# Windowed attention in a decoder: scores and values as one 64-row, 32-column matmul per head

## What is computed

```python
for i in range(DEPTH):                                   # 6 layers
    x = attn_layer(shift_tokens(x), Wqkv[i], q_scale[i], k_scale[i], Wo[i]) + x
    x = ffn_layer(shift_tokens(x), ln_g[i], ln_b[i], W1[i], b1[i], W2[i], b2[i]) + x

def attn_layer(x, Wqkv, qs, ksc, Wo):
    q, k, v = jnp.split(x @ Wqkv, 3, -1)                 # 16 heads of 64
    q, k = l2norm(q) * qs, l2norm(k) * ksc               # then rotary tables on both
    out = local_attention(q, k, v)
    return out @ Wo

def local_attention(q, k, v):                            # windows of 32, keys of this window and the last
    sim = jnp.einsum('bhwie,bhwje->bhwij', bq, bk2) * QK_SCALE
    attn = jax.nn.softmax(jnp.where(mask, -max, sim), -1)
    return jnp.einsum('bhwij,bhwje->bhwie', attn, bv2)
```

## Time and profile before

| | us |
|---|---|
| median of 3 runs | 2283.92 (2264.66 to 2285.11) |
| the profiled execution | 2264.08 |
| its span, first to last instruction | 2262.3 |
| PE busy | 2027.8 (90%) |
| DVE busy | 1530.3 (68%) |
| ACT busy | 1326.9 (59%) |
| POOL busy | 995.1 (44%) |
| mean granted TensorE clock | 0.962 of full speed |

### The profile page before, as it was taken

One profiled execution on the slowest core, in us unless ns is written; L12 is line 12 of the kernel. 1 busy time (PEld: TensorE's weight loads), 2 busy tenths in 40 slices (PEclk: granted clock), 3 DMA queues, 4 the chain that ended last, 5 costly groups with the idle time before them and its releaser, 6 DMA issues. The chain is left out here.

```text
span 2262.3 us, 46768 instructions
## 1 busy us (share of the span) xinstructions
PE 2027.8 (90%) x19016; PEld 1170.9 (52%) x19016; DVE 1530.3 (68%) x1741; ACT 1326.9 (59%) x1857; POOL 995.1 (44%) x715
## 2 busy tenths in 40 slices
PE   6799887589999999999999999999999999999996
PEld 2122133246656565555655565656555565556553
DVE  3989225466777677677777777767767777777762
ACT  3057764355665566656665666556665666566653
POOL 6000003165555555555555555555555555555540
PEclk8589998789999999999999999999999999999998
DMA  4510000034333343333443334433344333333331
GB/s 110 101 20 2 2 18 16 25 93 123 84 94 92 101 121 105 101 87 96 130 105 92 87 97 113 112 92 93 93 120 116 89 101 95 92 94 100 94 89 41
DMA packets 102357, 194.55 MB, mean 86 GB/s; under 512 B 12400, under 2 KB 32368, under 8 KB 102000
## 3 DMA queue, kind: packets, MB, share of 16 engines
q1 hardware_dynamic: 102144, 191.56, 32.4%
HBM read 123.77 MB, written 54.66 MB: 79 GB/s over the span
## 5 line engine op out<-in xcount | busy, mean ns | idle before, releaser
L1212 POOL TENSOR_TENSOR l_rot<-l_rot,l_rot_s 128x1024 f32<-128x1024 f32 x192 | 459.9, 2396 | 89.7 <-ACT l_norms L1413 64.9
L1527 DVE TENSOR_TENSOR l_rot<-ps,l_tab_c 128x1024 f32<-128x1024 f32 x192 | 235.2, 1225 | 313.2 <-PE ps L1248 195.5
L1215 POOL TENSOR_TENSOR l_rot<-l_rot,l_norms 128x1024 f32<-128x1024 f32 x192 | 365.3, 1903 | 15.1
L1201 POOL COPY l_kb<-l_kb 128x512 f32<-128x512 f32 x95 | 57.9, 610 | 709.4 <-ACT l_kb L1427 709.4
L1401 ACT ACTIVATE l_sq<-ps 128x1024 f32<-128x1024 f32 x192 | 196.8, 1025 | 221.7 <-PE ps L1239 219.1
L1539 DVE TENSOR_TENSOR l_rot_s<-ps,l_tab_s 128x512 f32<-128x512 f32 x384 | 245.6, 681 | 0.0
L1290 PE MATMUL ps<-l_vb,l_pT 128*32 128x128 f32 x6144 | 187.0, 273 | 65.0 <-ACT l_pT L1393 65.0
L1518 DVE TENSOR_REDUCE l_norms<-l_sq 128x16 f32<-128x1024 f32 x192 | 232.2, 1209 | 0.0
L1239 PE MATMUL ps<-l_wqkv,xsT 128*128 128x512 f32 x384 | 188.4, 615 | 26.6 <-ACT l_v_tok L1393 15.3
L1290 PEld LDWEIGHTS ps<-l_vb,l_pT 128*32 128x32 f32 x6144 | 165.9, 110 | 82.2 <-ACT l_pT L1393 82.2
L1410 ACT ACTIVATE l_norms<-l_norms 128x16 f32<-128x16 f32 x192 | 41.5, 216 | 279.6 <-POOL l_norms L1209 279.1
(11 more groups left out here) (165 smaller groups left out, 3352.1 us busy)
## 6 DMA issues: line engine op xcount, KB each, us to landing
l_vb<-v_scratch SPq DMA_DIRECT2D x336, 256.0 KB, 4.6
v_scratch<-l_v_tok SPq DMA_DIRECT2D x96, 512.0 KB, 4.8
l_vb<-v_scratch SPq DMA_DIRECT2D x48, 192.0 KB, 3.1
xsT<-xT SPq DMA_DIRECT2D x48, 135.8 KB, 2.5
stack<-scratch SPq DMA_DIRECT2D x96, 64.0 KB
l_xf<-xT SPq DMA_DIRECT2D x48, 128.0 KB, 2.3
l_wqkv_odd<-wqkv SPq DMA_DIRECT2D x9, 512.0 KB, 6.5
scratch<-parts SPq DMA_DIRECT2D x4, 768.0 KB, 11.4
```

What stands on the lines that cost most here:

```text
L1212: nc.gpsimd.tensor_tensor(rot[:, n], rot[:, n], rot_s[:, n], ALU.add).then_inc(added, 1)
L1215: nc.gpsimd.tensor_tensor(rot[:, n], rot[:, n], norms[:, t % 2, n, :, None].broadcast_to([P, HEADS, DH]), ALU.mult).then_inc(rotated, 1)
L1527: nc.vector.tensor_tensor(rot[:, 1 - r], slot(name, t).rearrange("p n (h d) -> p (n h) d", d=DH), tab_c[:, 1 - r, t % TILES, None, :].broa ...
```

## The change

`kb` and `vb` lose the parity axis: both heads' keys lie in the same columns, one head in partitions 0 to 63 and the other in 64 to 127, without zeros. `scores` and `values` issue two matmuls where one was, one per head, each with 64 rows, 32 columns and 64 moving columns; the even heads go to the slot's first bank and the odd heads to its second. The readers of these banks on DVE take the heads in the new order, and write `l_dif` and `l_o_tok` in the old one. The DMAs that spread v have the same source, size and number; their destination has no gap for the other parity. ACT copies kT with one ACTIVATE of 128 partitions, and takes the inverse norm of k behind the square of q and the copy of the probabilities.

```diff
-                    kb=sb("l_kb", [P, 2, PAIRS, 2, WINDOW + P]), vb=sb("l_vb", [P, WINDOWS, 2, PAIRS * DH]))
+                    kb=sb("l_kb", [P, 2, PAIRS, WINDOW + P]), vb=sb("l_vb", [P, WINDOWS, PAIRS * DH]))
...
-                            sp.dma_start(vb[r:r + WINDOW, j:, a, :], src.rearrange("(j r) x -> r j x", r=WINDOW))\
+                            sp.dma_start(vb[r:r + WINDOW, j:, :], src.rearrange("(j r) x -> r j x", r=WINDOW))\
...
-                    nc.gpsimd.tensor_copy(kb[:, t % 2, :, :, 0:WINDOW],
-                                          kb[:, (t - 1) % 2, :, :, P:P + WINDOW]).then_inc(carried, 1)
+                    nc.gpsimd.tensor_copy(kb[:, t % 2, :, 0:WINDOW],
+                                          kb[:, (t - 1) % 2, :, P:P + WINDOW]).then_inc(carried, 1)
...
                         for j in range(WINDOWS):
-                            a = j * WINDOW
-                            m = nc.tensor.matmul(dst[a:a + WINDOW, c // 4, (c % 4) * P:(c % 4 + 1) * P],
-                                                 qT[:, c, a:a + WINDOW], kb[:, t % 2, c, :, a:a + 2 * WINDOW],
-                                                 start=False, stop=True, skip_group_check=True)
+                            a, at = j * WINDOW, 2 * c * WINDOW
+                            for n in range(2):
+                                rows = slice(64 * n, 64 * n + 64)
+                                m = nc.tensor.matmul(dst[a:a + WINDOW, n, at:at + 2 * WINDOW],
+                                                     qT[rows, c, a:a + WINDOW], kb[rows, t % 2, c, a:a + 2 * WINDOW],
+                                                     start=False, stop=True, skip_group_check=True)
...
                         for j in range(WINDOWS):
-                            a = j * WINDOW
-                            m = nc.tensor.matmul(dst[a:a + WINDOW, c // 4, (c % 4) * P:(c % 4 + 1) * P],
-                                                 pT[:, c, a:a + WINDOW], vb[:, j, :, c * DH:(c + 1) * DH],
-                                                 start=True, stop=True, skip_group_check=True)
+                            a, cols = j * WINDOW, slice(c * DH, (c + 1) * DH)
+                            for n in range(2):
+                                rows = slice(64 * n, 64 * n + 64)
+                                m = nc.tensor.matmul(dst[a:a + WINDOW, n, cols], pT[rows, c, a:a + WINDOW],
+                                                     vb[rows, j, cols], start=True, stop=True, skip_group_check=True)
...
-                    src = slot("kT", t).rearrange("p n (c q) -> p (n c) q", q=P)
-                    for parity in range(2):
-                        rows = slice(64 * parity, 64 * parity + 64)
-                        m = nc.scalar.activation(kb[rows, t % 2, :, parity, WINDOW:], src[rows, :, :], ACT.Copy)
-                    m.then_inc(emptied("kT", t), 1)
+                    nc.scalar.activation(kb[:, t % 2, :, WINDOW:],
+                                         slot("kT", t).rearrange("p n (c q) -> p (n c) q", q=P), ACT.Copy)\
+                        .then_inc(emptied("kT", t), 1)
...
                     if has(t):
-                        inverse_norm(t, 0)
                         square(t, 1)
                     if has(t - 2):
                         copy_probs(t - 2)
+                    if has(t):
+                        inverse_norm(t, 0)
...
-                    nc.vector.tensor_tensor(dif[:, :, :], s,
-                                            mx[:, t % 2, :, None].broadcast_to([P, HEADS, 2 * WINDOW]),
+                    nc.vector.tensor_tensor(dif[:, :, :].rearrange("p (c n) k -> p n c k", n=2), s,
+                                            mx[:, t % 2, :, :, None].broadcast_to([P, 2, PAIRS, 2 * WINDOW]),
                                             ALU.subtract).then_inc(emptied("s", t), 1)
...
-                    nc.vector.tensor_tensor(o_tok[:, :, :], slot("o", t).rearrange("p n (h d) -> p (n h) d", d=DH),
-                                            inv[:, t % 2, :, None].broadcast_to([P, HEADS, DH]), ALU.mult)\
+                    nc.vector.tensor_tensor(o_tok[:, :, :].rearrange("p (c n) d -> p n c d", n=2),
+                                            slot("o", t).rearrange("p n (c d) -> p n c d", d=DH),
+                                            inv[:, t % 2, :].rearrange("p (c n) -> p n c", n=2)[:, :, :, None]
+                                            .broadcast_to([P, 2, PAIRS, DH]), ALU.mult)\
```

More of the change, by code:

```diff
@@ L834, in _ @@
                 pool.memset(env["xsT"][:, :, 0:1], 0.0).then_inc(zeroed, 1)
-                pool.memset(kept["kb"][:, :, :, :, :], 0.0).then_inc(zeroed, 1)
-                pool.memset(kept["vb"][:, :, :, :], 0.0).then_inc(zeroed, 1)
+                pool.memset(kept["kb"][:, :, :, :], 0.0).then_inc(zeroed, 1)
+                pool.memset(kept["vb"][:, :, :], 0.0).then_inc(zeroed, 1)
                 for t in range(NT):
@@ L986, in layers @@
         qT = sb("l_qT", [P, PAIRS, P])
-        mx = sb("l_mx", [P, 2, HEADS])
+        mx = sb("l_mx", [P, 2, 2, PAIRS])
         dif = sb("l_dif", [P, HEADS, 2 * WINDOW])
@@ L1556, in shift_scores @@
                 def shift_scores(t):
-                    s = slot("s", t).rearrange("p n (h k) -> p (n h) k", k=2 * WINDOW)
+                    s = slot("s", t).rearrange("p n (c k) -> p n c k", k=2 * WINDOW)
                     wait_full(dve, "s", t)
-                    nc.vector.tensor_reduce(mx[:, t % 2, :], s, AX.X, ALU.max).then_inc(maxed, 1)
+                    nc.vector.tensor_reduce(mx[:, t % 2], s, AX.X, ALU.max).then_inc(maxed, 1)
                     wait(dve, maxed, t + 1)
                     wait(dve, exped, t)
-                    nc.vector.tensor_tensor(dif[:, :, :], s,
-                                            mx[:, t % 2, :, None].broadcast_to([P, HEADS, 2 * WINDOW]),
+                    nc.vector.tensor_tensor(dif[:, :, :].rearrange("p (c n) k -> p n c k", n=2), s,
+                                            mx[:, t % 2, :, :, None].broadcast_to([P, 2, PAIRS, 2 * WINDOW]),
                                             ALU.subtract).then_inc(emptied("s", t), 1)
```

## The result

The changed kernel takes 2371.86 us (median of 4 runs, 2362.1 to 2377.82), the kernel before, run beside it, 2280.06 us (2264.66 to 2285.11). The ratio is 1.041, with a 95% interval of 1.0345 to 1.0476. It is slower by 4.1%, where 2112 us were forecast. The profiled execution took 2375.76 us.

What follows compares the result with a forecast made beforehand. PE was taken as the bound, with a small hole per step from ScalarE's order. Four steps sum to -6.45 us per batch, x 24 = -155: 2109, stated as 2112 us; own range 2085 to 2140, 8-in-10 range 2080 to 2225.

Steps and rivals of the forecast that it cites:

- So PE issues a pair in 7 to 11 ns: Scores and values on PE: issue time per load and matmul, read from bursts of eight weight loads.
- 128 x 8.5 = 1.09: New scores or values group: 128 pairs at 8.5 ns, plus 0.06 handover, 1.15 us; 1.33 us saved per step.
- no burst in the trace is longer than eight: Point noted in favour of a limit by instruction issue or fetching, in PE's scores and values.
- rival 2: Scores and values: instruction issue or fetching keeps each pair at 28 ns; 3.6 us per group, 2545 us; chance 0.16.
- 28 x 4 = 112: Scores and values: 112 ns nearly equals a 128-column pass, 109 ns, so columns explain the cost without a per-pair price.
- pT wait gone: PE's wait before values for ScalarE's copy of turned probabilities, 65.0 us in all, vanishes when the k norm moves.
- Row halves at the same time: Scores and values on PE: both 64-row halves of a column group run together; array bound 0.9 us per group.
- Rival 1: Scores and values: row halves take turns or PE looks ahead too little; groups stay 1.76 us, 2199 us; chance 0.18.
- One copy of kT: ScalarE: one 128-partition copy replaces two of 64 partitions, removing 1.03 us.
- The carry: POOL's carry moves half the elements: 0.61 us becomes some 0.33, bounds 0.3 and 0.61.
- The new order of reads on DVE, 0: DVE's maxima, differences and scaled outputs: same element count, so 0 change, bounds -0.1 and +0.3 us each.
- Late next in the hidden layer: Hidden layer step: PE's second group waits for DVE to free the scores' bank; 1.31 us stall, -0.88 left.

Runs made afterwards that it cites:

- e12: Changed kernel with the v projection moved between scores and values on PE (a repeat run): 2192.84 us, ratio 0.9632 to the kernel before.
- e5: Kernel before with the norm of k behind the pT copy and each scores and values matmul split in two of 64 columns: 2389.71 us, ratio 1.0484.
- half columns: Kernel before with the norm of k behind the pT copy, only even heads' scores and values computed: 2132.51 us, single run.

## Why the prediction was wrong

**The step that failed** is the one from a burst to a group: "So PE issues a pair in 7 to 11 ns", read from eight loads, and then "128 x 8.5 = 1.09". The rate within a group came out nearly so, 10 ns per pair. What fell is that a group gets its instructions at that rate. In its place the runs showed a supply of about 27 ns per pair over a page, and 207 us of stalls in 113 gaps; eight pairs are 16 of the 256 instructions of a page and could never show it. The text had the warning ("no burst in the trace is longer than eight") and gave rival 2 0.16.

**Rival 2** had the right cause by name ("fetching instructions") and side, in the wrong form. It made every pair take 28 ns, 3.6 us a group, 2545 us. In fact a group runs at 10 ns per pair until the page ends, and PE then stands, 1.84 us in the mean of the 113 gaps; with the eight records of the v projection between the dense groups (e12) 45 gaps with 41 us are left. So the loss is 207 us of stalls, not 2 x 1.8 x 96 = 346. My case against the rival, that 28 x 4 = 112 is the column price, was right (the runs with 64 columns show it) and didn't bear on it: the supply's 27 ns stood right beneath it, and the array's price hid it. The page of 256 instructions could be read in the trace of before, from q8's packets beside PE's records, and I didn't read it; how long a page takes at the least, that trace, which has no such gap, doesn't show.

**Point by point.**
- pT wait gone: right, and the order alone brings it, 74 us measured against 65.
- Row halves at the same time: right. 128 pairs of 64 rows in 1.29 us, where 128 pairs of 64 columns with all 128 rows took 1.87 (e5); in turns it would be 1.76 by the forecast's estimate. Rival 1 falls. A group was priced at 1.15 us in the forecast (the 0.06 for the handover in it was a guess that no run shows by itself), and takes 1.29 (with the values behind it) to 1.42 us (with a full-array matmul behind it) in the trace. With 1.29 for the scores and 1.42 for the values a fed step saves 3.63 - 2.71 = 0.92 us instead of 1.33, 88 us instead of 128 over 96 steps. The 1.42 is taken from the scores. The changed kernel has hardly a values group without a gap, and in e12 those without one take 1.55 us in the median (1.41 at the least). With 1.55 it is 0.79 us a step, 76 us.
- One copy of kT: right, one L1427 of 1.04 us per tile. The carry takes 0.40 us, forecast 0.33.
- The new order of reads on DVE, 0: right, 1.22 us for L1561 as for its ancestors.
- Late next in the hidden layer: right in kind, too large. It is seen once the stalls are small, 0.44 us behind `l_dif` where 1.31 were forecast, in 8 batches of 24.
- The price of instructions over a page: no term, +207 us.
- The clock: no term. Behind a stall the granted clock fell in some steps, as in the one above: 1.00 up to the 2.37 us hole, then the trace's lower level, 0.50, for 3.4 us from 1165.85 on. The mean of the second window is 0.54, that of 1166 to 1168 alone 0.50. The v projection runs there; its matmuls of 512 columns take up to 1.22 us each, against 0.60 in the median of the run (L1316). The columns of the two windows are those of the earlier trace rows:

```profile
1161.00:1165.40 4.40, 1.77 (x161) 1.61 (x161) 4.37 (x6) 0.52 (x2) 4.32 (x4) 1.00 0.02 4
1165.60:1168.80 3.20, 3.20 (x5) 1.25 (x5) 1.38 (x2) 0.00 (x0) 3.12 (x2) 0.54 0.55 140
```

By my own sum over the layers PE was at 0.50 for 26 us before, 159 after, and 23 to 47 in the kernels with v between. Of the 41 such stretches after, 30 begin within 4 us behind a gap; but only 35 of the 113 gaps are followed by one, and in the split columns 3 of 109. The 133 us more cost at most half of it, 66 us, since what runs at 0.50 takes twice as long (1.22 against 0.60 us).

The sum with measured terms: 2280 - 74 (order) - 88 (groups) + 207 (stalls) = 2325, or 2337 with the 76 for the groups, and 0 to 66 for the clock: 2325 to 2403, where 2372 was measured. What part of the clock's share is real isn't settled: no run took it apart from the stalls. The split columns have little of it (43 us at 0.50); the same sum gives 2204 + 159 = 2363 for them, and 2390 was measured, so some 27 us of it are unexplained there.

## What to carry to other kernels

Before matmuls are made smaller and more numerous, divide PE's records by 256 and ask how long the densest 256 of them take: here one page took some 3.5 us in the median, and groups that would have used it up sooner stalled in some of their steps: the changed kernel's (256 in 1.29 us, 207 us of stalls), the split columns' (1.87 us, 159 us) and the half columns' (some 2.1 us, 22 us). The same two groups stalled for 207 us side by side and for some 45 us with 1.8 us of large matmuls between, so dense stretches are to be kept apart by work with few instructions, with as few changes of shape as may be (one more change cost 0.24 us here). The best versions run are the changed kernel with v between (0.9637 and 0.9632) and the one with the new scores only and v between (0.9613 and 0.9638), which can't be told apart; both beat both kernels. The new order of ScalarE alone gives 0.968 and 0.967.

## What the runs showed of the hardware

- PE's instructions came 256 at a time: 248 packets of 16 KB for 63626 records, 152 for 39050. Where PE stalled in the changed kernel, the next page's transfer began about 1.0 us after PE entered the current one, took 1.1 us, and PE went on 1.35 us after it had landed (medians): some 3.45 us, 13.5 ns per instruction, and never under 3.55 us where PE had stood at both ends of a page. In that trace the next page landed 2.3 us behind PE's entry into the current one in the median (1.4 us ahead of it at the earliest), and the page after it never sooner than 3.6 us behind, so I found no sign of more than one page on hand ahead.
- With instructions on hand, f32 matmuls of 64 rows, 32 columns and 64 moving columns followed each other over eight tiles at 10 ns per pair of load and matmul (1.29 us for 128), both row halves and all four column groups in use and the two halves in two banks. With 128 rows, 64 columns took 14.6 ns per pair (1.87 us for 128, split columns).
- One more change from column groups to the full array and back cost 0.24 us (5.69 against 5.45 us for the same three groups).
- The granted clock stood at 1.00 or 0.50. Behind the 2.37 us hole it was at 0.50 for 3.4 us; behind most stalls it didn't fall: it did behind 35 of 113 gaps in the changed kernel and 3 of 109 in the split columns.
